# A four-layer cross-attention kernel: transposed tiles moved to multiples of 512 bytes, two small steps moved to ScalarE, instruction orders changed

## What is computed

```python
def gqa(x, cond):                       # layers 0 and 2
    xn = rmsnorm(x, norm_w)
    q, k, v = xn @ wq, cond @ wk, cond @ wv        # 16, 4, 4 heads of 8
    attn = softmax(q k^T / sqrt(8))                # [16, 128, 77]
    return x + (attn @ v) @ wo
def mha(x, cond):                       # layers 1 and 3
    q, k, v = x @ Wq, cond @ Wk, cond @ Wv         # 16 heads of 64
    attn = softmax(q k^T / 8 + col_bias)
    return (attn @ v) @ Wo + bo + x
```

## Time and profile before

| | |
|---|---|
| median of the runs | 1936.2 us |
| profiled execution | 1937.2 us, its span 1934.6 us |
| TensorE busy | 1813.3 us, 94% |
| VectorE, ScalarE, GpSimd busy | 84%, 74%, 78% |
| DMA | 320.31 MB, mean 166 GB/s |
| mean granted TensorE clock | 0.973 |

### The profile page before, as it was taken

The page is one execution under the profiler, slowest core; times in us unless marked ns, Lnnn a source line. Parts: engine busy times, 40 slices in busy tenths (PEclk is TensorE's granted clock), DMA queues, the critical chain, the costliest instruction groups (busy, mean ns, idle before and its releaser), DMA issues.

```text
span 1934.6 us, 72375 instructions
## 1 busy us (share of the span) xinstructions
PE 1813.3 (94%) x28144; PEld 1567.9 (81%) x28272; DVE 1622.0 (84%) x3322; ACT 1422.5 (74%) x2539; POOL 1508.7 (78%) x1880
## 2 busy tenths in 40 slices
PE   5699999999999999999999999999999999999995
PEld 5578888888888888888888888888888888888874
DVE  7688988898888998888888988888888898888873
ACT  3477777777877777777777777777877777777762
POOL 3478887788878888888888888788887888888863
PEclk7699999999999999999999999999999999999997
DMA  5289999999999999999999999999999999999995
GB/s 163 53 144 168 172 174 168 174 159 174 170 174 171 179 173 175 175 170 172 174 174 178 170 170 172 171 166 174 166 173 174 171 170 169 164 172 171 164 167 109
DMA packets 1168206, 320.31 MB, mean 166 GB/s; under 512 B 1140246, under 2 KB 1164124, under 8 KB 1167868
## 3 DMA queue, kind: packets, MB, share of 16 engines
q1 hardware_dynamic: 1167868, 315.69, 99.4%
HBM read 15.93 MB, written 4.19 MB: 10 GB/s over the span
## 4 chain that ended last, share of the span: by engine, by line
PE 68%; SPq 12%; DMA 6%; POOL 4%; issue 4%; DVE 2%; ACT 2%; ACTq 0%; POOLq 0%
PE ring L1205 36%; PE sc L1342 8%; SPq L485 6%; PE o_ps L1205 6%; DMA arena<-arena 5%; PE ring L1414 4%; PE o_ps L1360 4%; PE sc L1325 3%; SPq L517 2%; SPq L471 2%; PE sc L1340 1%; PE ring L1400 1%; SPq L504 1%; POOL p_sm L640 1%; PE ring L1276 1%
## 5 line engine op out<-in xcount | busy, mean ns | idle before, releaser
L635 POOL TENSOR_TENSOR p_sg<-arena,p_sg 128x512 f16<-128x512 f32 (+1 forms) x256 | 347.7, 1358 | 195.4 <-ACT p_sg L702 195.3
L1205 PE MATMUL ring<-ctx_four,m_w 128*128 128x154 f16 x6144 | 463.8, 230 | 0.8 <-DVE v_tile L898 0.6
L1205 PEld LDWEIGHTS ring<-ctx_four,m_w 128*128 128x128 f16 x6144 | 427.2, 96 | 1.5 <-DVE v_tile L898 0.8
L1080 DVE TENSOR_TENSOR arena<-sc,row_max 128x616 f32<-128x616 f32 (+2 forms) x512 | 407.0, 795 | 8.9
L640 POOL TENSOR_TENSOR p_sm<-arena,p_sm 128x616 f16<-128x616 f32 x256 | 337.8, 1320 | 40.5 <-ACT p_sm L702 40.4
L702 ACT ACTIVATE arena<-ring 128x462 f16<-128x462 f32 (+1 forms) x384 | 196.5, 512 | 182.0 <-PE ring L1205 181.9
L663 POOL TENSOR_TENSOR arena<-arena 128x1024 f16<-128x1024 f32 x128 | 273.9, 2140 | 17.7 <-ACT arena L702 17.7
L1205 PE MATMUL ring<-wv_m,ctx_four 128*103 128x512 f16 (+1 forms) x1152 | 280.1, 379 | 0.2
L1342 PE MATMUL sc<-arena,x_s 128*128 128x512 f16 (+1 forms) x1152 | 262.2, 336 | 6.8
L1059 DVE TENSOR_TENSOR arena<-ring,arena 128x462 f16<-128x462 f32 (+1 forms) x384 | 222.5, 579 | 14.3 <-ACT arena L702 9.0
L1077 DVE TENSOR_REDUCE row_max<-sc 128x6 f32<-128x462 f32 (+2 forms) x384 | 225.0, 586 | 6.0 <-PE sc L1342 4.9
(11 more groups left out here) (165 smaller groups left out, 3702.3 us busy)
## 6 DMA issues: line engine op xcount, KB each, us to landing
v_fourth<-v_tile SPq DMA_DIRECT2D x64, 105.6 KB
ctx_nat<-in_ctx_dram SPq DMA_DIRECT2D x64, 77.0 KB
x_nat<-in_x_dram SPq DMA_DIRECT2D x64, 64.0 KB, 2.6
arena<-p_sg SPq DMA_TRANSPOSE x256, 4.0
arena<-p_sm SPq DMA_TRANSPOSE x256, 4.8
out_dram<-y_out SPq DMA_DIRECT2D x64, 64.0 KB, 2.3
v_fourth<-v_tile SPq DMA_DIRECT2D x32, 101.6 KB
arena<-in_L_xattn_Wk_dram SPq DMA_DIRECT2D x2, 1024.0 KB, 5.9
```

The lines of the kernel that those rows point to most:

```text
L635: pool.tensor_tensor(p_sg[k][:, LO, 0:e - a], probs_flat[:, a:e], p_sg[k][:, HI, 0:e - a], ALU.subtract).then_inc(sems["pg_lo"], 1)
L1080: dve.tensor_tensor(shifted[:, hs, :], s_view[:, hs, :], row_max[:, hs].unsqueeze(2).to_broadcast([P, hs.stop - hs.start, S]), ALU.subtrac ...
L1205: ins = pe.matmul(out, a, b, start=(n == 0), stop=(n == len(passes) - 1))
```

## The change

Four things are changed.

1. Places in SBUF. A pad `to_512`, `p_sm`, `p_sg` and the arena are now declared first, and inside the arena the transposes' tiles (p_tm, p_tg, o_s, o_t) come first. Each of these then starts at a multiple of 512 bytes in its partition. Before, p_sm and p_sg started 416 bytes past one, and p_tm, p_tg, o_s and o_t 320 bytes past one.
2. `first_x` goes from VectorE to ScalarE.
3. The two heads of `normalise_m(.., 1)` are no longer multiplied by VectorE in one instruction; VectorE takes the reciprocals, and ScalarE scales them with two activations (`normalise_rest`).
4. The orders in `pair` of all five engines and in `ring_uses` change. rest_and_turn goes from the start of a pair to the end of the pair before; scores_g goes ahead of output_m; the three folded chunks follow one another; the MHA scores go ahead of the first value chunk; turn_out goes ahead of move_values; spread_keys goes behind both low parts of g.

```diff
+        sb("to_512", [P, 96], F32)
+        p_sm = sb("p_sm", [P, 2, 2, HALF, P], F16)
+        p_sg = [sb(f"p_sg{k}", [P, 2, (b1 - b0) * P], F16) for k, (b0, b1) in enumerate(G_BLOCKS)]
+        arena = sb("arena", [P, ARENA], F32)
...
         taken[0] = 0
+        p_tm = in_arena(2 * H * T, F16).rearrange("p (k a h t) -> p k a h t", k=2, a=2, t=T)
+        p_tg = [in_arena(2 * (b1 - b0) * T, F16).rearrange("p (a b t) -> p a b t", a=2, t=T) for b0, b1 in G_BLOCKS]
+        o_s = in_arena(2 * NOC * P, F16).rearrange("p (a n) -> p a n", a=2)
+        o_t = in_arena(2 * NOC * T, F16).rearrange("p (a c t) -> p a c t", a=2, t=T)
+        o_n = in_arena(NOC * P, F32)
         g_s = [in_arena(4 * HS, F16).rearrange("p (a t h s) -> p a t h s", a=2, t=2, s=S) for n in range(2)]
...
 # SyncE, pair
                     turn_m(it, m - 2, 1)
+                if exists(it, m - 4):
+                    turn_out(it, m - 4)
                 if exists(it, m - 2) and part(m - 2) != 3:
                     move_values(it, m - 2)
-                if exists(it, m - 4):
-                    turn_out(it, m - 4)
...
 # GpSimd, pair
                     low_out(it, m - 4)
+                if exists(it, g + 4):
+                    x_parts(it, g + 4)
                 if exists(it, g):
                     low_part(it, g, 0)
                 if layer(g + 4) == 0 and part(g + 4) == 3 and exists(it, g + 4):
                     context_parts(it, g + 4)
+                if exists(it, g):
+                    low_part(it, g, 1)
                 if exists(it, g + 2):
                     spread_keys(it, g + 2)
                 if exists(it, g):
-                    low_part(it, g, 1)
-                if exists(it, g + 4):
-                    x_parts(it, g + 4)
-                if exists(it, g):
                     pack_values(it, g)
-                if exists(it, m):
-                    low_part(it, m, 0)
                 if exists(it, m + 2):
                     x_parts(it, m + 2)
                 if exists(it, m):
+                    low_part(it, m, 0)
                     low_part(it, m, 1)
...
 # ScalarE, new
+            def first_x(it, n, g):
+                b = ring_bank(n, ("ct", g, 0))
+                act.wait_ge(sems["ct_raw"], at("ct_raw", it, g, 1))
+                high(x_f[stream(g)][:, :], ring[:, b, X_IN], 1.0).then_inc(sems["xg_f32"], 1)
+
+            def normalise_rest(it, n, m):
+
+                act.wait_ge(sems["om_rcp"], at("om_rcp", it, m, 2))
+                act.wait_ge(sems["om_norm"], at("om_norm", it, m, 1))
+                for h in range(*O_PARTS[1]):
+                    ins = act.activation(o_n[:, h * MD:(h + 1) * MD], om_rest(ring_bank(n, ("ot", m - 1, 0)))[:, 0, h - O_PARTS[1][0], 0:MD],
+                                         ACT.Copy, scale=den_r[:, H + h:H + h + 1])
+                ins.then_inc(sems["om_norm"], 1)
```

```diff
-                if exists(it, g - 4) or exists(it, m - 4):
-                    rest_and_turn(it, n, g - 4)
+                if exists(it, g):
+                    scores_g(it, g)
                 if exists(it, m - 6):
                     output_m(it, n, m - 6)
-                if exists(it, g):
-                    scores_g(it, g)
                 if exists(it, lead):
                     folded(it, n, lead, chunks[0])
                     folded(it, n, lead, chunks[1])
+                    folded(it, n, lead, chunks[2])
+                if exists(it, g - 2):
+                    values_g(it, g - 2)
+                if exists(it, g + 2):
+                    keys_values(it, n, g + 2)
                 if layer(g + 4) == 0 and exists(it, g + 4):
                     turn_inputs(it, n, g + 4)
...
+                for j, k in value_chunks(n)[0:1]:
+                    if exists(it, j):
+                        context_values(it, n, j, k)
+                if exists(it, g - 4):
+                    output_g(it, n, g - 4)
                 if exists(it, m - 2):
                     values_m(it, m - 2)
-                if exists(it, g - 4):
-                    output_g(it, n, g - 4)
                 for j, k in value_chunks(n)[1:2]:
                     if exists(it, j):
                         context_values(it, n, j, k)
+                if exists(it, g - 2) or exists(it, m - 2):
+                    rest_and_turn(it, n, g - 2)
```

More of the change, by code:

```diff
@@ L849, in pair @@
                     folded(it, n, lead, chunks[1])
+                    folded(it, n, lead, chunks[2])
+                if exists(it, g):
+                    exponential_g(it, g, 0)
+                if exists(it, g + 2):
+                    keys_values(it, n, g + 2)
+                if layer(g + 4) == 0 and exists(it, g + 4):
+                    first_x(it, n, g + 4)
+                if exists(it, g):
+                    high_g(it, g, 0)
                 if layer(g + 4) == 0 and exists(it, g + 4):
@@ L852, in pair @@
                 if exists(it, g):
[L853 to L858, removed]
-                if exists(it, g):
                     exponential_g(it, g, 1)
                     high_g(it, g, 1)
+                    picked_values(it, n, g)
+                if exists(it, g + 2):
+                    queries(it, n, g + 2)
                 for j, k in value_chunks(n)[0:1]:
@@ L1029, in _ @@
             fold_low(1)
[L1031 to L1034, removed]
             def turn_context(it, n, g):
@@ L1122, in normalise_m @@
                     dve.wait_ge(sems["o_lo"], at("o_lo", it, m - 2, 1))
+                if k == 1 and exists(it, m - 2):
+                    dve.wait_ge(sems["om_norm"], at("om_norm", it, m - 2, 2))
                 dve.reciprocal(r, o[:, :, :, MD:MD + 1]).then_inc(sems["om_rcp"], 1)
+                if k == 1:
+                    return
                 dve.wait_ge(sems["om_rcp"], at("om_rcp", it, m, k + 1))
@@ L1151, in pair @@
                     finish_m(it, n, m - 6)
+                if exists(it, g):
+                    shift_g(it, g, 1)
                 if exists(it, lead):
                     folded(it, n, lead, chunks[0])
-                if layer(g + 4) == 0 and exists(it, g + 4):
-                    first_x(it, n, g + 4)
-                if exists(it, lead):
                     folded(it, n, lead, chunks[1])
-                if exists(it, g):
-                    shift_g(it, g, 1)
-                if layer(g + 4) == 0 and exists(it, g + 4):
-                    turn_context(it, n, g + 4)
+                    folded(it, n, lead, chunks[2])
                 if exists(it, g - 2):
                     normalise_g(it, g - 2)
-                if exists(it, m):
-                    maximum_m(it, m, 0)
-                if exists(it, lead):
-                    folded(it, n, lead, chunks[2])
                 if exists(it, g + 2):
@@ L1170, in pair @@
                 if exists(it, m):
+                    maximum_m(it, m, 0)
+                if layer(g + 4) == 0 and exists(it, g + 4):
+                    turn_context(it, n, g + 4)
+                if exists(it, m):
                     maximum_m(it, m, 1)
                     shift_m(it, m, 0)
+                    maximum_m(it, m, 2)
+                    shift_m(it, m, 1)
+                if exists(it, g + 2):
+                    queries(it, n, g + 2)
                 for j, k in value_chunks(n)[0:1]:
@@ L1428, in pair @@
                     folded(it, n, lead, chunks[1])
+                    folded(it, n, lead, chunks[2])
+                if exists(it, g - 2):
+                    values_g(it, g - 2)
+                if exists(it, g + 2):
+                    keys_values(it, n, g + 2)
                 if layer(g + 4) == 0 and exists(it, g + 4):
                     turn_inputs(it, n, g + 4)
-                if exists(it, g - 2):
-                    values_g(it, g - 2)
-                if exists(it, lead):
-                    folded(it, n, lead, chunks[2])
                 if exists(it, m):
                     scores_m(it, m, 0)
-                if exists(it, g + 2):
-                    keys_values(it, n, g + 2)
-                if exists(it, m):
                     scores_m(it, m, 1)
-                for j, k in value_chunks(n)[0:1]:
-                    if exists(it, j):
-                        context_values(it, n, j, k)
                 if exists(it, g):
```

39 lines of the change are left out of this document (11 added, 28 removed).

## The result

The changed kernel takes 1852.8 us (1852.26 to 1853.76), the kernel before 1937.1 us in the same comparison: a ratio of 0.957, 95% interval 0.9546 to 0.9594. The forecast was 1906 us with a range of 1872 to 1945; the direction was right, the time lies 19 us under the range.

What follows compares the result with a forecast made beforehand. TensorE's own work plus one wait, for turned_o in output_m, was taken as the bound. 1937.2 - 28.6 (steady stops) - 3 (early stops) + 1 (k_bd) = 1906.6, median 1906 us; own range 1892 to 1920, overall 1872 to 1945.

Steps and rivals of the forecast that it cites:

- the sum: Whole kernel: 1937.2 - 28.6 - 3 + 1 = 1906.6 us, given as 1906 us for the median.
- the stops for turned_o: TensorE ahead of output_m, steady stretch: 42.1 us in 42 stops, of which 28.6 us were to go.
- the alignment: Transpose tiles moved to multiples of 512 bytes: taken as 0 us; bounds from 0 to removal of all waits, no loss.
- rival 1: DMA transposes: unaligned rows cost, p_sm's take 0.63 us less, every turned_o stop goes; 1886 us (1872 to 1895), chance 0.30.
- TensorE's busy time changing by itself: Steady stretch: named sign that the prediction was wrong, alongside a fall in the granted clock; no size given.
- turn_out before move_values: SyncE's order: output's transpose issued ahead of the copy to v_fourth, 1.01 us slack for turned_o in three pairs of four.
- scores_g before output_m: TensorE's order: moves the deadline of turned_o by 0.72 us, less 0.2 us for a later y_out.
- normalise_rest: Scaling of last two MHA heads: VectorE loses 0.29 us, ScalarE gains two copies of 0.22 us each; cost 0.
- k_bd: GpSimd's spread_keys later: slack 1.5 us before scores_g, 0.2 us in shorter pairs; priced 0 to 32 us, taken as 1.
- rival 3: GpSimd and scores_g: k_bd comes late and TensorE stands at the pair's start; 1952 us, up to 1975, chance 0.12.
- Its sign: TensorE at scores_g: a wait sc<-POOL k_bd would show that late k_bd slows the kernel; no size given.
- Rival 2: SyncE's DMA queue is the true bound, so stops move to values_m and values_g; 1928 to 1940 us, chance 0.13.

## Why the prediction was wrong

Right was what bounds the kernel: TensorE and one wait, for turned_o. With the old places the orders give 31 us, and the sum had 30.6. That agreement is partly luck: the stops for turned_o fell from 40.3 to 19.1 us where 28.6 of 42.1 were to go, the two neighbourhoods of float32 matmuls, 17 us, weren't in the sum, nor were 14.4 us of waits for p_sm and p_sg.

1. The step that failed is the alignment, taken at 0 us; it measured 69 us alone and 52 on top of the orders. The argument was that the same addresses show two rates, 199 to 219 and 270 to 292 GB/s, so that the slower is not the address's alone. But two limits can hold one after the other: a transpose that was held shows only the second, the movement of data, and the one that was not shows the first. That the address enters at the first fits the runs. Two rates at one address say that there is a second condition, not that the address is harmless. The sound reading was that the unqueued rate had no row at another address, with rival 1's price as the open end and its chance above 0.30.
2. The rule of the Trainium skill (the page "DMA: Bandwidth & Descriptors", section "How a descriptor splits into AXI transactions") pointed the right way: it says that the bytes ahead of a start off a multiple of 256 are fetched and cost beats. The beats it counts did not come out in this case's traces: 32 and 224 bytes past cost p_sm the same. The row that was held against it, 5.4 us for the output's transpose and 4.8 for p_sm's, compared medians of two tiles that both crossed; their shortest landings were 4.3 and 4.2 us, and both are 3.6 in the changed kernel.
3. Rival 1 was the right mechanism and was sized at 1886, with a range down to 1872. It took 0.63 us off each p_sm transpose (3.6 instead of 4.2 us was measured) and let every stop of the steady stretch go, which is what happened. The new places alone, 1866.5, are 20 us under it. It counted the stops that the profile names (47 us) and 4 at the end. By the timelines the new places save 52 us in the 96 steady pairs alone, whose named stops are 37.6, and 11 us behind them.
4. The steady state's own TensorE work was taken as fixed. It was not: 256 x (315 - 274) ns and 256 x (241 - 212) ns, 17.9 us, went by a change of neighbours. "TensorE's busy time changing by itself" was named as a way to be wrong, but no price was put on it.
5. turn_out before move_values gives 1.01 us of slack in three of four pairs; that was put at 22 us and alone gave 26. scores_g before output_m was put at 24 and gave 14.
6. normalise_rest: each activation takes 306 ns, not 0.22 us, and more than the 128x128 copy of 270:

```profile
L745 ACT ACTIVATE arena<-ring,den_r 128x64 f32<-128x64 f32 x218 | 55.7, 306 | 12.4 <-DVE den_r L1137 12.4
```

It cost nothing, as said, since nothing waits for it.
7. k_bd: it was put at 1.5 us ahead of the boundary in the pair shown, 0.2 in the shorter ones. In the pair below it ends at 1326.29, and scores_g starts its sum of squares at 1328.71: 2.4 us. Between 280 and 1760 us the smallest distance is 0.96 us, so rival 3 did not come about there. Its sign did appear at the start, before 100 us, where TensorE stops twice at scores_g for k_bd, 6.0 us in all, a price that the sum hadn't (the timeline, then TensorE's wait from 0 to 100 us):

```profile
1325.59 0.70 POOL L650 TENSOR_TENSOR k_bd<-k_mix,group_mask 128x308 f16<-128x308 f16 x1
...
1328.71 0.28 PE L1327 MATMUL sc<-ones,x_sq 128*128 128x1 f32 x2
```

```profile
PE sc L1335 <- POOL k_bd L650: 6.0, 2, 3.4
```

8. Rival 2 (a full DMA queue) holds only at the old places, in part. At the new ones SyncE's queue waits for GpSimd's p_sm 189.4 us between 280 and 1760 us, against 84.9 between 280 and 1840 before:

```profile
SPq L479 <- POOL p_sm L641: 189.4, 108, 2.7
```

## What to carry to other kernels

Start every source tile of a DMA transpose at a multiple of 256 bytes in its partition; it costs one pad and here it was worth 69 of 84 us. When a resource shows two rates under conditions that the trace can't hold apart, give the untested condition its full price as a rival instead of arguing it to zero. And once TensorE waits for nothing, look at which matmul stands beside each float32 one, since its cost changed here by 26 to 41 ns with its neighbour, 256 times over, and check that the new order brings no wait for a bank, as it did in four of the six runs made on this.

## What the runs showed of the hardware

- A DMA transpose of 0.52 MB with 256-byte source rows, issued into an empty queue, landed in 3.6 us at least when its rows started at a multiple of 256 bytes and in 4.2 us when they started 32, 160 or 224 bytes past one. The target's address (0 or 320 past 512) made no difference that shows in the landings, and a multiple of 512 none over 256. For the shortest p_sg transposes (0.26 MB) it was 2.7 us against 3.0 to 3.1.
- Of the 256-byte packets of these transposes 1.2% took over 30 ns with rows on multiples of 256, and 8.7 to 9.3% with crossing rows.
- After a stall the crossing rows moved at 270 to 292 GB/s, about the aligned ones' 286 to 294; into an empty queue they moved at 199 to 219.
- Float32 matmuls of 128 columns took a mean 315 ns behind 65-column float16 products and 274 ns behind 512-column ones; a float32 transpose 316 ns behind 48-column and 284 ns behind 154-column ones. That it is the length of the product ahead which hides part of the float32 weight load was only argued from these.
